# Value products of attention in groups of three steps instead of two

## The reference

```python
x = x + attn_a(layernorm(x))      # 16 heads of 16, causal, ALiBi bias, projections with bias
x = x + ffn(layernorm(x))         # mixture of 8 experts, top 2
x = x + attn_b(layernorm(x))      # 16 heads of 16, causal, rotary positions
x = x + ffn(layernorm(x))

scores = einsum('bhqd,bhkd->bhqk', q, k) * scale + bias
attn   = softmax(scores)
out    = einsum('bhqk,bhkd->bhqd', attn, v)
```

## Time and profile before

| | us |
|---|---|
| median of 3 runs (3921.8 to 3924.3) | 3923.59 |
| the profiled execution | 3924.12 |
| its span, first to last instruction | 3922.3 |
| TensorE matmuls busy | 3808.2 |
| VectorE busy | 2955.1 |
| ScalarE busy | 2759.2 |
| GpSimd busy | 1060.0 |

### The profile page before, as it was taken

One profiled execution on the slowest core, in us unless ns is written; L12 is line 12 of the kernel. 1 busy time (PEld: TensorE's weight loads), 2 busy tenths in 40 slices (PEclk: granted clock), 3 DMA queues, 4 the chain that ended last, 5 costly groups with the idle time before them and its releaser, 6 DMA issues.

```text
span 3922.3 us, 109333 instructions
## 1 busy us (share of the span) xinstructions
PE 3808.2 (97%) x42692; PEld 2394.3 (61%) x42693; DVE 2955.1 (75%) x3839; ACT 2759.2 (70%) x5702; POOL 1060.0 (27%) x1794
## 2 busy tenths in 40 slices
PE   7999999999999999999999999999999999999998
PEld 5555555555656656556875556556655665557955
DVE  7788888888888888885048888888888888884075
ACT  2777777777777777776257777777777777775265
POOL 4121112222222234442024333333333332120021
PEclk9999999999999999999999999999999999999999
DMA  5333233333333333335644333343343334246622
GB/s 164 73 77 83 55 88 87 77 77 90 79 92 92 91 105 100 95 105 163 229 142 111 99 91 92 102 104 97 86 104 96 88 87 95 68 87 196 222 73 87
DMA packets 275748, 407.05 MB, mean 104 GB/s; under 512 B 65226, under 2 KB 190098, under 8 KB 262418
## 3 DMA queue, kind: packets, MB, share of 16 engines
q1 hardware_dynamic: 272158, 391.66, 37.7%
q0 software_dynamic: 3072, 8.39, 0.8%
HBM read 264.70 MB, written 122.13 MB: 99 GB/s over the span
## 4 chain that ended last, share of the span: by engine, by line
PE 49%; DVE 2%; ACT 2%; DMA 1%; issue 1%; SPq 1%; POOL 1%; ACTq 0%; DVEq 0%; POOLq 0%
PE ps_acc L1261 14%; PE ps_r L1198 10%; PE ps_p L1230 9%; PE ps_p L1386 4%; PE ps_r L1398 4%; PE ps_r L1322 2%; ACT probs L1079 2%; DVE part_max L1592 1%; PE ps_r L1203 1%; PE ps_r L1307 1%; PE ps_p L1224 1%; PE ps_r L1317 1%; PE ps_r L1308 1%; PE ps_r L1309 1%; PE ps_p L1237 1%
## 5 line engine op out<-in xcount | busy, mean ns | idle before, releaser
L1592 DVE TENSOR_REDUCE part_max<-ps_p 128x2 f32<-128x1024 f32 (+3 forms) x2560 | 2623.1, 1060 | 578.1 <-PE ps_p L1230 391.8
L1079 ACT ACTIVATE probs<-ps_r 128x512 f32<-128x512 f32 (+1 forms) x4608 | 2334.2, 575 | 688.8 <-PE ps_r L1198 432.8
L1198 PE MATMUL ps_r<-q_stack,k_stack 54*128 54x512 f32 (+3 forms) x5120 | 1378.1, 392 | 38.0 <-ACT probs L1079 28.7
L1230 PE MATMUL ps_p<-k_stack,q_stack 52*128 52x512 f32 (+3 forms) x5120 | 1249.2, 428 | 25.4 <-DVE part_max L1592 22.9
L1261 PE MATMUL ps_acc<-probs,v_head 128*17 128x256 f32 x19456 | 1146.7, 361 | 1.8 <-ACT probs L1079 1.6
L1198 PEld LDWEIGHTS ps_r<-q_stack,k_stack 54*128 54x128 f32 x5120 | 733.2, 187 | 267.0 <-ACT probs L1079 219.9
L1261 PEld LDWEIGHTS ps_acc<-probs,v_head 128*17 128x17 f32 x19456 | 489.6, 97 | 468.0 <-issue 218.4
L1230 PEld LDWEIGHTS ps_p<-k_stack,q_stack 52*128 52x128 f32 x5120 | 558.6, 186 | 297.2 <-DVE part_max L1592 155.7
L1203 PE MATMUL ps_r<-id,mk 64*128 64x64 bf16 x3598 | 284.1, 194 | 0.0
L1713 DVE COPY xf<-ps_r 128x256 f32<-128x256 f32 x46 | 19.5, 424 | 316.2 <-PE ps_r L1398 316.2
L1030 POOL TENSOR_TENSOR bk<-bk,y_sb 128x256 f32<-128x256 f32 x104 | 76.2, 733 | 658.2 <-ACT y_sb L1130 658.1
(11 more groups left out here) (198 smaller groups left out, 3155.0 us busy)
## 6 DMA issues: line engine op xcount, KB each, us to landing
q_stack<-parts SPq DMA_DIRECT2D x378, 128.0 KB
k_stack<-parts SPq DMA_DIRECT2D x378, 128.0 KB
parts<-pa SPq DMA_DIRECT2D x128, 256.0 KB, 2.6
parts<-pb SPq DMA_DIRECT2D x128, 256.0 KB, 3.3
probs<-w_dram SPq DMA_DIRECT2D x30, 1024.0 KB, 6.1
o_sums<-acc_sb SPq DMA_DIRECT2D x1008, 17.0 KB
swp<-tmp SPq DMA_DIRECT2D x128, 128.0 KB, 3.1
bk<-recips SPq DMA_DIRECT2D x58, 256.0 KB
```

Of the source, the lines that this page charges most:

```text
L1079: act.activation(probs[:, at % PBUF, u, 0:w], block_bank(g, n, u)[:, 0:w], ACT.Exp)\
L1198: mm = pe.matmul(bank[:, col:col + QW - q0], ks[s][r, kb * P:(kb + 1) * P], qs[s][r, qt * QW + q0:(qt + 1) * QW], start=fresh, stop=True, ...
L1230: mm[u] = pe.matmul(banks[:, u, col:col + w], qs[s][r, qb * P:(qb + 1) * P], ks[s][r, kc * QW:kc * QW + w], start=fresh, stop=True, skip_g ...
L1592: mm = dve.tensor_reduce(part_max[:, :, qb, kc], ps_p[:, p1_banks(g, n), col:col + w], AX_X, ALU.max)
```

## The change

```diff
@@ value_groups
     for qt in reversed(range(NQ)):
         at = [n for n, slot in enumerate(STEP) if slot[0][0] == qt]
         while at:
-            n = 3 if len(at) == 3 else 2
+            n = 2 if len(at) in (4, 5, 7) else 3
             groups.append(at[:n])
             at = at[n:]
     return groups
```

## The result

| | before | after |
|---|---|---|
| median, us | 3922.7 (3920.3 to 3924.3) | 4075.7 (4071.5 to 4087.0) |
| ratio, 95% interval | | 1.040 (1.038 to 1.042) |
| span of the profiled execution, us | 3922.3 | 4071.6 |
| forecast, us | | 4066 (4015 to 4125) |

The kernel is 4% slower. The forecast was 10 us short of the median, and inside its range.

The account below looks back on a forecast made before the run. TensorE was taken as the bound. Per pair, 2.58 us of moved steps less 0.92 saved plus 0.56 of added waits gave 2.22 us; 64 pairs gave 142 us, so 4066 us, range 4015 to 4125.

Parts of the forecast that it names:

- TensorE as the bound, priced by its stream: Slots 2, 3, 4, 6, 9, 10 each grow by one 0.43 us step on TensorE's path: 2.58 us a pair added.
- The ring in place of the removed group: At emptied slots 1, 5, 11, three score banks awaiting ScalarE limit the saving to 0.92 us a pair.
- The replay: Exponential ends set against next bank users in emptied slots 1, 5, 11: saved 0.08, 0.30, 0.54 us.
- The late groups: Groups of slots 4 and 10 wait for their last step's exponential, 0.28 us each: 0.56 us a pair added.
- What was costed at nothing: The probabilities' six buffers and the evacuations of ps_acc were to cost nothing, since PE's instruction order hides or keeps them.
- The stretches without a side job: 22 of the 192 removed slots, where VectorE sets the pace; not priced apart, about 12 us less at the low end.
- The edges win: First bank free before the fourth score: each removed slot gives 1.08, costs 0.86; 42 us faster, 3882 us; chance 0.06.
- Its price of 1.08: Full saving in us per removed slot, group with its edges, if nothing else held PE.
- Nothing gained or lost: Edges free and banks holding nobody up: two moved steps cost 0.86 and free 0.86, 3924 us; chance 0.03.
- VectorE as a second brake: Unit bursts behind emptied slots overload VectorE: 0.4 us in each of 192 stretches, 77 us on top, 4143 us; chance 0.08.
- The signs that were named: Profile after: about 200 more score waits near 0.5 us, some 120 value waits near 0.3, a pair 2.2 us longer.

Follow-up runs that it names:

- Experiments 5: Kernel before, with the three exponentials ahead of each of slots 1, 5 and 11 cut from 512 to 128 columns, except in the first pair: 3957.7 us, ratio 1.000.
- Experiment 6: Changed kernel, with the three exponentials ahead of each of slots 1, 5 and 11 cut from 512 to 128 columns, except in the first pair: 4035.8 us, ratio 1.019.
- Experiment 3: Changed kernel with step 8 moved from slot 4's group to slot 6's, and step 20 from slot 10's to slot 12's: 4028.6 us, 1.028 of the kernel before.
- experiments 4: Changed kernel with the next step's two scores issued ahead of the unit where the odd slot is empty: 4068.4 us, 1.038 of the kernel before.
- experiment 7: Kernel before with its empty slots 7 and 17 filled by one-step groups, 18 groups in all: 3932.2 us, ratio 0.995.

## Why the prediction was right, point by point

**TensorE as the bound, priced by its stream.** Right. Six steps at 0.43 us: each grown group that nothing else disturbs costs 0.428 to 0.430 (slots 2 to 3, 6 to 8), and no idle time of PE absorbed any of it.

**The ring in place of the removed group.** Right in mechanism and in the pace. The replay gave 0.92 us a pair for the three slots, and 0.157 + 0.264 + 0.489 = 0.91 was measured (0.43 less the table's entries for slots 5 and 11). The three parts are off in ways that cancel. Slot 1 was priced at 0.08 on the premise that everything behind the job is unchanged. The job did begin 1345.88 - 1344.25 = 1.63 us after the first exponential, as replayed (1.58 + 0.06), but behind it the last score follows its unit after 0.23 us (1347.37 to 1347.60), where before the group of slot 2 began 0.63 after such a unit (1299.14 to 1299.77) and now 0.54 (1347.37 to 1347.91). That 0.09 is the part that the premise left out, and the weight loads show what it was. In the kernel before, the weight load of that unit waits for VectorE; in the kernel after it doesn't:

```profile
1299.12 0.18 PEld L1230 LDWEIGHTS ps_p<-k_stack,q_stack 52*128 52x128 f32 x2 [0.21 <-DVE part_max L1592]
```

```profile
1347.13 0.19 PEld L1230 LDWEIGHTS ps_p<-k_stack,q_stack 52*128 52x128 f32 x2
```

In the kernel before this load waits over 0.1 us in 47 of 60 pairs, and there two scores on either side of the unit are 0.545 us apart in the median, otherwise 0.47; in the kernel after it waits in 7 of 57. The unit behind the removed group now begins 1.49 us after the first unit (1343.42 to 1344.91), not 1.89 (1295.11 to 1297.00), so VectorE gets its work sooner and is done sooner. Over the span the waits of these loads for VectorE fell from 155.7 us to 105.3. The prediction saw VectorE as harmless and missed that the change would help it.

Slots 5 and 11 each gave 0.04 to 0.05 less than replayed. In pair 22, from the fourth score at slot 11 to the job are 1.22 us (1376.48 to 1377.70) where the replay kept 1.14; at slot 5 the job begins 0.14 after the third exponential's end (1356.98 + 1.58 = 1358.56), not 0.06. Why is not shown. That the three add up to 0.91 is luck.

Experiments 5 and 6 show the mechanism from the other side: shorten only the exponentials that hold the ring, and the change costs 78 us instead of 153, while the kernel before doesn't move.

**The late groups.** Right: 0.28 + 0.28 forecast, 0.28 + 0.29 measured. The replay of the exponential had given 0.35 for slot 10; taking 0.28 for both was the better choice, but it was a guess between rows. Experiment 3 removes them alone and gets the 0.57 us back.

**What was costed at nothing.** The stretches from slot 12 to 18 have a median difference of 0, as has 8 to 9. The buffers of the probabilities and the evacuation of ps_acc held nobody up.

**The stretches without a side job.** Left unpriced, they changed little: 21 of the 22 can be compared between the traces (the first pair has nothing ahead of its slot 1), and they come to 3.8 us less than as many medians would.

**The 10 us that are missing.** 143 of 153 us are in the table, and 6 us of the rest lie in the profiled spans. Summed instead of taken as medians, the stretches come to 152.5 us, 10 more than the table's 143, above all where groups grew (slots 2 to 3 and 6 to 8, 5 us each). The mean granted clock fell from 0.995 to 0.989; in the traces that is 42 us of the one span and 92 of the other at 1.2 GHz, the rest at 2.4. The 30 stretches in which one of the two traces shows 1.2 GHz lie 16 us above their medians; all others together lie 7 us below. Slots 6 to 8 of pair 6, first after, then before (stretch and its length, busy time by engine, granted clock, DMA):

```profile
461.52:469.75 8.23, 7.68 (x66) 4.33 (x63) 5.05 (x6) 4.38 (x10) 1.49 (x8) 0.79 0.13 33
```

```profile
448.93:455.12 6.19, 5.63 (x57) 3.45 (x55) 5.07 (x6) 4.38 (x10) 1.38 (x7) 1.00 0.19 45
```

2.04 us more instead of 0.43, with PE busier by as much and VectorE and ScalarE unchanged. So the clock accounts for what the spans have beyond the medians. The prediction had no term for it, and why the change spends more time at 1.2 GHz is not shown. The last 4 us, from the spans to the medians of the runs, are no more than the runs of the change differ among themselves.

**The rivals.** *The edges win* failed where the prediction put its deciding point, at the fourth score. A free PE comes there 0.48 us after the first of the three scores (1295.44 to 1295.92, the prediction's working), thus at 1344.24; the first exponential was over at 1344.85. Experiment 6 adds that short exponentials don't bring it about: even at 0.28 us a removed slot gave 0.70 to 0.80, so with 0.86 of stream moved elsewhere the change would still not have paid. Its price of 1.08 was not tested, since 0.35 us of stop were left. *Nothing gained or lost* needed free edges and free banks; neither is there. *VectorE as a second brake* did not come: its reductions (by line: busy, mean ns, idle time before them and who ended it) stood idle longer for PE than before, first the kernel before, then the one after.

```profile
L1592 DVE TENSOR_REDUCE part_max<-ps_p 128x2 f32<-128x1024 f32 (+3 forms) x2560 | 2623.1, 1060 | 578.1 <-PE ps_p L1230 391.8
```

```profile
L1592 DVE TENSOR_REDUCE part_max<-ps_p 128x2 f32<-128x1024 f32 (+3 forms) x2560 | 2637.0, 1060 | 715.3 <-PE ps_p L1230 560.5
```

It is next in line, though: experiments 4 and 6 met it as soon as the ring was eased.

**The signs that were named.** Waits at the scores were to grow by 200 places or more of 0.5 us. They grew by 163 (from 175 to 338 over both lines, with 13.2 us in 56 places at L1194 before), fewer than named, with 0.51 us each. The waits of value groups (some 120 of 0.3 us forecast, 130 of 0.27 found), the job at 1.6 us, the 1.4 us for 24 records and the 2.2 us for a pair came as written.

## What to carry to other kernels

In this kernel, work that needs no bank of the small ring is the cover under which the ring is emptied. Merging such work into larger groups saves edges only if the ring's releaser can follow without the cover: before counting the edges, replay the releaser's first, second and third end against the next users' starts, from its own rows. Where a stream already has places without cover, the gain lies in cutting the covering work finer and filling them, and behind the first brake one should look at once for the next.

## What the runs showed that was not expected

The start of an exponential costs nearly as much as its length. It begins 0.49 us after the first of its scores, with 512 columns or 128, and ends 0.60 or 0.28 us later; chained ones are 0.49 apart. The hand-over to a matmul that waits for an exponential is 0.05 to 0.06 us in all 468 places of the trace after, and in all 178 before.

Taking a group out relieved VectorE: the next unit reaches it 0.40 us sooner, and the waits of PE's weight loads for it fell by a third.

The same kernel takes different times on different chips, with the granted clock: the kernel before 3920 us at 0.993 to 0.995 and 3955 at 0.986 to 0.993, and in ten runs of experiment 7 the time went from 3916.7 at 0.992 to 3952.2 at 0.982. A difference of one per cent had to be taken from runs on the same chip.
